# One core of attention and mixture of experts: scores moved to two 64-row halves of the array

## The reference

```python
q = rmsnorm(x @ q_a_w.T, q_a_ln) @ q_b_w.T          # 16 heads of 64 (plain) + 64 (rotary)
ckv = x @ kv_a_w.T                                   # latent c of 32, rotary key of 64, one for all heads
kv = rmsnorm(c, kv_a_ln) @ kv_b_w.T                  # keys 64 and values 128 per head out of the 32
scores = einsum('bhsd,bhtd->bhst', query, key) / sqrt(128)
attn = softmax(scores)                               # over all 2048 keys, no mask
out = einsum('bhst,bhtd->bhsd', attn, v) @ o_w.T
```

## Time and profile before

| | |
|---|---|
| median of the runs | 2390.89 us |
| the profiled execution | 2386.19 us |
| its span, first to last instruction | 2384.4 us |
| TensorE busy | 2140.0 us, 90% |
| VectorE, ScalarE, GpSimd busy | 1511.3, 1375.4, 1338.5 us |
| mean granted TensorE clock | 0.942 |

### The profile page before, as it was taken

The page is one execution under the profiler, slowest core; times in us unless marked ns, Lnnn a source line. Parts: engine busy times, 40 slices in busy tenths (PEclk is TensorE's granted clock), DMA queues, the critical chain, the costliest instruction groups (busy, mean ns, idle before and its releaser), DMA issues. The chain is left out here.

```text
span 2384.4 us, 38677 instructions
## 1 busy us (share of the span) xinstructions
PE 2140.0 (90%) x10554; PEld 1421.9 (60%) x10554; DVE 1511.3 (63%) x3046; ACT 1375.4 (58%) x1927; POOL 1338.5 (56%) x762
## 2 busy tenths in 40 slices
PE   5896999999999999999999999999873659999990
PEld 3643666666666666666666666666553436777760
DVE  4536777777777777777777777777142324555557
ACT  2521677777777777777777777767731214555540
POOL 1001777777777777777777777777725331333330
PEclk8886999999999999999999999999986879999995
DMA  4119990000000000000000000000012244999987
GB/s 158 53 29 370 402 396 7 0 0 0 0 0 0 0 0 0 0 0 0 0 0 0 0 0 0 0 0 1 1 49 81 67 145 142 337 357 343 345 281 249
DMA packets 90336, 227.35 MB, mean 95 GB/s; under 512 B 13198, under 2 KB 46904, under 8 KB 90040
## 3 DMA queue, kind: packets, MB, share of 16 engines
q1 hardware_dynamic: 77240, 195.03, 23.1%
q0 software_dynamic: 10752, 29.72, 3.3%
q10 hardware_dynamic: 2304, 2.10, 0.3%
HBM read 125.52 MB, written 101.28 MB: 95 GB/s over the span
## 5 line engine op out<-in xcount | busy, mean ns | idle before, releaser
L632 POOL TENSOR_TENSOR prob_lo<-prob,prob_hi 128x1024 f16<-128x1024 f32 x512 | 1108.3, 2176 | 435.8 <-ACT prob_hi L651 425.8
L649 ACT ACTIVATE prob<-p_s,prob_scale 128x1024 f32<-128x1024 f32 x512 | 571.4, 1116 | 463.2 <-PE p_s L798 456.9
L684 DVE TENSOR_REDUCE maxes<-p_m 128x1 f32<-128x512 f32 x1024 | 700.7, 691 | 120.5 <-PE p_m L771 103.8
L651 ACT ACTIVATE prob_hi<-p_s,prob_scale 128x1024 f16<-128x1024 f32 x512 | 567.3, 1108 | 0.0
L771 PE MATMUL p_m<-k_hi,q_hi 96*128 96x512 f32 x1024 | 420.5, 414 | 10.4 <-DVE maxes L684 7.7
L798 PE MATMUL p_s<-q_hi,k_hi 97*128 97x512 f32 x1024 | 360.0, 433 | 5.5 <-ACT prob_hi L651 3.9
L798 PE MATMUL p_s<-q_lo,k_hi 97*128 97x512 f32 x1024 | 323.6, 397 | 0.0
L798 PE MATMUL p_s<-q_hi,k_lo 97*128 97x512 f32 x1024 | 323.1, 397 | 0.0
L1059 POOL DMA_INDIRECT ranked_out<-y,dest x128 | 122.8, 959 | 265.7 <-DVE y L1363 258.4
L771 PEld LDWEIGHTS p_m<-k_hi,q_hi 96*128 96x128 f32 x1024 | 195.4, 191 | 91.4 <-DVE maxes L684 34.8
L798 PEld LDWEIGHTS p_s<-q_hi,k_hi 97*128 97x128 f32 x1024 | 171.4, 189 | 121.2 <-issue 67.9
(11 more groups left out here) (231 smaller groups left out, 2259.0 us busy)
## 6 DMA issues: line engine op xcount, KB each, us to landing
w<-in_experts SPq DMA_DIRECT2D x128, 608.0 KB
expert_rows<-zeros SPq DMA_DIRECT2D x129, 526.0 KB, 9.1
rows<-expert_rows SPq DMA_DIRECT2D x128, 131.5 KB
got<-ranked_out SPq DMA_DIRECT2D x16, 768.0 KB, 11.1
wqb<-in_wqb SPq DMA_DIRECT2D x16, 341.0 KB, 3.0
x<-in_x SPq DMA_DIRECT2D x1, 2048.0 KB, 8.5
cbar<-in_woT SPq DMA_DIRECT2D x1, 2048.0 KB
ranked_out<-y,dest POOLq DMA_INDIRECT x128
```

Source lines behind the costliest of these rows:

```text
L632: gp.tensor_tensor(prob_lo[s % NB][:, :], prob[s % 2][:, :], prob_hi[s % NB][:, :], ALU.subtract).then_inc(lo_ready, 1)
L649: act.activation(prob[s % 2][:, :], p_s[s % 2][:, :], ACT.Exp, bias=prob_scale[:, :], scale=SCALE)
L651: act.activation(prob_hi[s % NB][:, :], p_s[s % 2][:, :], ACT.Exp, bias=prob_scale[:, :], scale=SCALE).then_inc(p_ready, 1)
L684: v.tensor_reduce(maxes[:, n:n + 1], p_m[n % 2][:, :], AX.X, ALU.max).then_inc(max_used, 1)
```

## The change

- Keys and queries lie on partitions in two halves of 64. Half c holds query chunk c of 512. `kr_hi`, `kr_lo` are the rotary key on both halves; `kc_pair` holds the 32 rounded latent rows and the 32 rows of their rest; `kc_one` the 32 rounded rows and a row of ones.
- A score tile is five products per half (64, 64, 64, 64 and 33 rows) in place of three on 96 or 97 rows. Half 0 and half 1 are issued in turn, into different banks.
- A maximum is two products per half (rotary, latent pair). 32 maxima are made in a pass as before, 16 on each half, the halves at different slots.
- `p_m` and `p_x` become one ring of three banks, through which maxima, the turn, the projections and the rows go in one order (36 uses a pass).
- The groups are eight: scores of two key tiles, then values of two.
- The projection is now two steps, `rope` and `rest`, each for both chunks, written to two column halves of 64. VectorE then works on 128 partitions. The rows step is one, of 33 columns.
- The norm's root scales `hT` in place of `cosq` and `sinq`. GpSimd splits the keys. Three copies of `wq` on ScalarE in place of one, earlier in the head.

```diff
-        q_hi = [sb("q_hi0", 2 * QC, F32R), sb("q_hi1", 2 * QC, F32R)]
-        q_lo = [sb("q_lo0", 2 * QC, F32R), sb("q_lo1", 2 * QC, F32R)]
+        kr_hi, kr_lo, kc_pair, kc_one = keys
+        qr_hi, qr_lo, qc_hi, qc_lo = ([sb(f"{name}{u}", QC, F32R) for u in range(2)] ...)
-        p_m = [pb("p_m0"), pb("p_m1")]
-        p_x = pb("p_x")
+        ring = [pb(f"ring{n}") for n in range(RING)]          # RING = 3
+        PARTS = ((kr_hi, qr_hi, ROPE), (kr_hi, qr_lo, ROPE), (kr_lo, qr_hi, ROPE), (kc_pair, qc_hi, 2 * C),
+                 (kc_one, qc_lo, KR))                          # KR = 33
+        SLOTS = BATCH * len(PARTS)                             # BATCH = 2
+        MORE, LESS, NONE = ((0, 4, 7), (2, 5, 9)), ((1, 6), (3, 8)), ((), ())
+        MAX_AT = (MORE, LESS, MORE, MORE, LESS, MORE, NONE, NONE)
         def plan(g, first=False, more=True, after=True):
+            rounds, at, done, open_max = [], [0, 0], list(BEGUN[g]), [False, False]
+            while min(at) < SLOTS or any(open_max):
+                now = []
+                aside = {(1, 0): ("turn", not first), (6, 8): ("rows", more)}.get((g, len(rounds)))
+                if aside and aside[1]:
+                    now.append((aside[0], None, None, None))
+                for c in range(2):
+                    places = MAX_AT[g][c][done[c] - BEGUN[g][c]:] if more else ()
+                    if open_max[c]:
+                        now.append(("max", c, done[c], 1))
+                        open_max[c], done[c] = False, done[c] + 1
+                    elif places and places[0] == at[c]:
+                        now.append(("max", c, done[c], 0))
+                        open_max[c] = True
+                    elif at[c] < SLOTS:
+                        now.append(("score", c, BATCH * g + 2 + at[c] // len(PARTS), at[c] % len(PARTS)))
+                        at[c] += 1
+                rounds.append(now)
+            if after and g in (5, 6):
+                rounds.append([({5: "rope", 6: "rest"}[g], None, None, None)])
...
# VectorE
+            def project_rope(half, use, bank):
+                step.mark(v.tensor_tensor(qr_raw[:, :], bank[:, :], cosq[:, tok], ALU.mult))
+                for n, (dst, src) in enumerate(((HALF, 0), (0, HALF), (ROPE + HALF, ROPE), (ROPE, ROPE + HALF))):
+                    turned = v.tensor_tensor(rot[dst:dst + HALF, :], bank[src:src + HALF, :], sinq[src:src + HALF, tok], ALU.mult)
...
+                step(v.tensor_tensor(qr_raw[:, :], qr_raw[:, :], rot[:, :], ALU.add))
+            def split(m, half, use, bank, first=False):
+                    v.wait_ge(s_mm, 16 * m - 16)
+                step.mark(v.tensor_copy(qr_hi[half][:, :], qr_raw[:, :]))
+                v.wait_ge(ring_mm, use + 1)
+                v.tensor_copy(qc_hi[half][:, :], bank[:, :]).then_inc(q_ready, 1)
+                step(v.tensor_tensor(qr_lo[half][:, :], qr_raw[:, :], qr_hi[half][:, :].bitcast(F32), ALU.subtract))
+                v.tensor_tensor(qc_lo[half][:, :], bank[:, :], qc_hi[half][:, :].bitcast(F32), ALU.subtract)...
# TensorE
+            def project(side, half, use, bank):
+                pe.wait_ge(ring_used, use + 1)
                 for k in range(DK):
+                    for c in range(2):
+                        last = pe.matmul(bank[c * ROPE:(c + 1) * ROPE, :], wq[:, k * P + side * ROPE:k * P + (side + 1) * ROPE],
+                                         hT[:, k * S + (2 * half + c) * QC:k * S + (2 * half + c + 1) * QC], ...)
+            def score(c, kt, part, m, half, rows_use):
+                kk, qq, n = PARTS[part]
+                b = slice(c * ROPE, c * ROPE + n)
+                done = pe.matmul(p_s[kt % 2][:, c * QC:(c + 1) * QC], kk[b, kt * P:(kt + 1) * P], qq[half][b, :], ...)
...
-                    for kt in range(4 * g, 4 * g + 4):
+                    for kt in range(BATCH * g, BATCH * g + BATCH):
                         weigh(kt, m)
```

More of the change, by code:

```diff
@@ L64, in __call__, with mark, settle @@
         self.now += 1
+        self.engine.wait_ge(self.semaphore, self.before + self.now)
+    def mark(self, instruction):
+        instruction.then_inc(self.semaphore, 1)
+        self.now += 1
+    def settle(self):
         self.engine.wait_ge(self.semaphore, self.before + self.now)
@@ L578, in attention @@
         vec = sem("vec")
-        def plan(g, first=False, more=True, after=True):
[L582 to L596, removed]
@@ new lines, in attention, with use_of @@
+        EVENTS = [what if c is None else (c, n) for g in range(len(MAX_AT)) for now in plan(g) for what, c, n, part in now
+                  if c is None or (what == "max" and part == 1)]
+        MAXIMA = [(c, n) for g in range(len(MAX_AT)) for now in plan(g) for what, c, n, part in now if what == "max" and part == 1]
+        USES = len(EVENTS)
+        def use_of(m, what, first=False, more=True, after=True):
+            place = EVENTS.index(what)
+            if first and place < EVENTS.index("turn"):
+                place += 1
+            if not after and place > EVENTS.index("rope"):
+                place -= 1
+            if not more:
+                place = -2
+            return USES + USES * m + place, ring[place % RING]
@@ L729, in _ @@
-            step(v.tensor_copy(identr[:, :], ident[:, :]))
-            for c in range(2):
-                project(0, c, 0, c)
-            for n in range(MX):
-                maximum(n, 0)
-            for c in range(2):
-                row(c, 0, 2 + c)
-            project(1, 0, 1, 4)
+                state = (first, more, after)
+                if not first:
+                    copy_out(m - 1)
+                for g in range(len(MAX_AT)):
+                    for now in plan(g, first, more, after):
+                        for what, c, n, part in now:
+                            if what == "max" and part == 1:
+                                maximum(c, n, m + 1, *use_of(m, (c, n), *state), (c, n) == MAXIMA[-1])
+                            elif what == "turn":
+                                turn(1 - half, h - (1 - half), *use_of(m, "turn", *state))
+                            elif what == "rows":
+                                rows(m + 1, 1 - half, *use_of(m, "rows", *state))
+                            elif what == "rope":
+                                project_rope(half, *use_of(m, "rope", *state))
+                            elif what == "rest":
+                                split(m + 2, half, *use_of(m, "rest", *state))
@@ new lines, in project_rest, with maximum @@
+            def project_rest(half, use, bank):
+                project(1, half, use, bank)
+            def maximum(c, n, part, m, half, use, bank):
+                j, kc = n // 4, n % 4
+                kk, qq = ((kr_hi, qr_hi), (kc_pair, qc_hi))[part]
+                if part == 0:
+                    if n == 0:
+                        pe.wait_ge(q_ready, 2 * m + 1)
+                    pe.wait_ge(ring_used, use + 1)
+                b = slice(c * ROPE, (c + 1) * ROPE)
+                last = pe.matmul(bank[:, :], qq[half][b, j * P:(j + 1) * P], kk[b, kc * QC:(kc + 1) * QC],
+                                 start=(part == 0), stop=(part == 1))
+                if part == 1:
+                    last.then_inc(ring_mm, 1)
@@ L797, in scores @@
-                for j in range(2):
-                    last = pe.matmul(p_s[kt % 2][:, j * QC:(j + 1) * QC], kk[0:KS, keys],
-                                     qq[half][0:KS, j * QC:(j + 1) * QC], start=(part == 0), stop=(part == 2))
-                if part == 2:
-                    last.then_inc(s_mm, 1)
+                if part == len(PARTS) - 1 and first_of_two and kt == 0:
+                    pe.wait_ge(ring_used, rows_use + 1 + RING)
+                kk, qq, n = PARTS[part]
+                b = slice(c * ROPE, c * ROPE + n)
@@ L803, in weigh @@
+                done = pe.matmul(p_s[kt % 2][:, c * QC:(c + 1) * QC], kk[b, kt * P:(kt + 1) * P], qq[half][b, :],
+                                 start=(part == 0), stop=(part == len(PARTS) - 1))
+                if part == len(PARTS) - 1 and not first_of_two:
+                    done.then_inc(s_mm, 1)
             def weigh(kt, m):
```

361 lines of the change are left out of this document (190 added, 171 removed).

## The result

The changed kernel takes 2270.33 us (median of 4 runs, 2267.98 to 2273.43) against 2389.72 (2385.43 to 2391.69). The ratio is 0.9503, 95% interval 0.9485 to 0.9522: 119 us or 5.0% faster. The forecast was 2310 and 81 us.

What follows compares the result with a forecast made beforehand. TensorE's stream was taken to set 31 of 32 passes. -2.33 us a pass gives -72, the last pass -4 and the start -5: -81 in all, so a median of 2310 us, range 2250 to 2380.

Steps and rivals of the forecast that it cites:

- the slots: TensorE's scores and maxima: 128 slots become 112 pair slots at 0.232 us each, -3.71 us a pass.
- rival D: Score pairs on TensorE: the halves don't overlap at all, +26 - 2.3 us a pass, 3120 us; chance 0.02.
- rival C: Score pairs on TensorE: the halves share the way of the weights; half way, 0.306 us a pair, 2568 us; chance 0.15.
- Rival A: Pairs on TensorE: as cheap as a value pair, 0.218 instead of 0.232 us, -3.3 a pass, 2280 us; chance 0.20.
- Rival B: New waits and dearer batches eat most: -1.0 us a pass, 2351 us, or 2379 with a fetch every jump; chance 0.14.
- The batches: Values on TensorE: four batches a pass become eight, 0.32 us extra each, +1.28 us a pass (+0.8 to +1.8).
- The wait for GpSimd: TensorE waits for GpSimd before values in short groups and after groups without maxima: +0.4 us a pass (0 to +1.2).
- The ring: Three banks in place of two let VectorE's maxima lag without holding TensorE: -0.2 us a pass (-0.7 to +0.6).
- Turn and rows: On TensorE the turn's four matmuls stay at 0.41 us; two row steps become one: -0.1 us a pass.
- VectorE's chain: VectorE's work after `rope` takes some 9 us, hidden by a thin margin before maxima 10 us after `rope`.
- The last pass: Pass without maxima, which waited for other engines in batches of four tiles; pairs smooth that: about -4 us.
- The start: Start of the attention: one full-height projection before the first maximum, rows once in place of twice: -5 us (-8 to +3).

Runs made afterwards that it cites:

- one_half: The changed kernel with both halves' score products reading partitions 0 to 63, same instructions and banks: 2865.16 us, ratio 1.1971 to the kernel before.
- fours: The changed kernel with values in fours of key tiles in the first three quarters of a pass (groups of 4, 4, 4, 2, 2): 2319.93 us.
- old_fastmax: The kernel before with each VectorE maximum taken over 256 of its 512 columns: 2383.14 us, ratio 0.9964.
- ring2: The changed kernel with a ring of two banks in place of three: 2364.18 us, ratio 0.9878 to the kernel before.
- serial: The changed kernel, but in a pass's last two groups each key tile's five products of half 0 come before the five of half 1: 2297.24 us.

## Why the prediction was right, and what it missed

- **What bounds, and the slots.** Right in what was counted: TensorE's stream sets a pass before and after, and 112 rounds at 0.231 us replace 128 slots. The forecast had 0.232 by analogy with column halves; one_half shows the overlap is all of the gain (+18.6 us without it for the scores alone), so rival D and, with a pair at 0.231 and not 0.30, rival C fell. The estimate of 0.302 a pair, from the 3.07 times in the Trainium skill, "TensorE: Matmul & The Clock Gate", section "Measured speedup vs the span model", doesn't hold for this stream of two row halves.
- **Rival A** gave 2280, nearest to the measured time, but by a mechanism that didn't happen: the pair didn't get as cheap as a value pair (0.231, not 0.218). **Rival B** went the other way: waits disappeared, and no jump waited for a fetch.
- **The batches.** The price of 0.32 held (0.31), four more times a pass.
- **Projection.** Right at 0: 1.77 us each (1006.93 to 1008.70), eight records in four pairs.
- **The term that was missing: the waits inside the old stream.** The prediction wrote that the other engines matter only if they are late for the new stream, and never added the old pass up from its own prices. 128 x 0.232 + 48 x 0.218 + 4 x 0.32 + 3.4 + 0.41 + 2 x 0.24 is 45.7 us of 46.97; the 1.2 that are over are for the most part the waits for ScalarE (0.33), VectorE (0.36) and the turn (0.29). The forecast credited 0.2 of them. Even the 8.70 us that gave the upper bound of a batch's price, 0.44, hold 0.16 of the wait for ScalarE (1012.55 to 1013.41). fours brings ScalarE's wait back.
- **The wait for GpSimd** was charged with +0.4 and shows no cost: 2.2 us of weight loads in three passes against 2.1 before, and the first values of a batch start 0.32 to 0.33 us behind the scores at each of the 12 batches of a trip that follow scores. No run speeds GpSimd up, so this rests on the starts alone. The margin of the hand calculation was thin and fell to the good side.
- **The ring.** -0.2 stood for VectorE's waits, which were 0.24 (old_fastmax) to 0.36 (starts); inside its bounds of -0.7 and +0.6. But they described a side matter, and ring2 shows that 2.84 us depend on the third bank.
- **Turn and rows.** The rows gave about the -0.1 that was forecast. The turn's four matmuls did not "stay": with the 0.29 of waiting gone and 0.59 us held in their new place (1019.32 to 1019.91), where they took 0.41 and made the next start 0.08 late, they cost about 0.2 less.
- Together, against the forecast of a pass: ScalarE -0.33, the turn -0.2, VectorE -0.1 to -0.2, GpSimd -0.4, the rounds -0.1 (0.231 in place of 0.232). That makes -1.1 to -1.2; the gap was -1.21. These are read from single distances and were not each tested alone. So the forecast's mechanism held, and it came out a third too small by waits that it had not counted.
- **VectorE's chain** ended, as forecast, just in time: the last rounding at 969.9, the copy out at 970.68, which waits 0.79 for the last values. It has no more than this in hand.

```profile
969.21 0.69 DVE L751 TENSOR_TENSOR qc_lo<-ring,qc_hi 128x512 fp32r<-128x512 f32 x1
970.68 0.69 DVE L775 COPY att_t<-p_o 128x512 f32<-128x512 f32 x1 [0.79 <-PE p_o L907]
```

- **The last pass** -3.4 (forecast -4). **The setup**, forecast at nothing, moved the first projection by 0.55 us (181.86 to 182.41). **The start** gave about -2.2 (-5.2 to the first copy, less one pass and the setup), forecast -5: the first rotation starts 3.0 us behind its projection in place of 2.1, and the pairs of maxima still come every 1.6 us, as before. **Instructions:** no packet ran between 400 and 1500 us, and no cost of the longer loop body shows.

## What to carry to other kernels

When an engine is over 99% busy, its own stream still can hold small waits for others. Add the old stream up from your unit prices first; what is left over (1.2 us of 46.97 here) holds its waits, and a change of order can take them away or bring more. A run that shortens one engine's work moves the other engines' waits too, so its gain is not the price of one wait. An edit of the batch size can be a loss alone (+62 us here) and necessary beside another one (fours, +50 us without it), because the faster stream meets the other engines' buffers at another moment. Before crediting an overlap, keep the instructions and take only the disjoint rows away; before crediting a buffer, remove it again.

## What the hardware showed that I had not expected

Matmuls of different row halves don't have to be neighbours in the program to overlap: in serial a product that stands sixth in the program started 0.22 us before the third, and ordering halves in blocks of five cost 0.87 us a pass in place of 4.6. A change of the array's shape delays the next start by about 0.1 us, in either direction, and also from 33 to 64 columns.
